# Graph attention and experts on one core: the query product of the second edge layer moves between a slot's two additions, and GpSimd gets 2 steps of 16

## What is computed

```python
Q = (enh @ Wq + bq).reshape(N, H, D); K = ...; V = ...      # H = 4 heads of D = 64
rel = rel_w[edge_relations]
mod_k = K[src] + 0.2 * rel[:, None, :]
scores = jnp.einsum('ehd,ehd->eh', Q[dst], mod_k) / D ** 0.5
seg_max = jax.ops.segment_max(scores, dst, num_segments=N)
ex = jnp.exp(scores - seg_max[dst])
denom = jax.ops.segment_sum(ex, dst, num_segments=N)
agg = jax.ops.segment_sum(ex / denom[dst] * V[src], dst, num_segments=N)
```

## Time and profile before

| what | value |
|---|---|
| median of 3 runs | 1919.19 us (1916.95 to 1919.61) |
| the profiled execution | 1912.22 us |
| its span, first to last instruction | 1910.5 us |
| busy over the span | DVE 1426.3 us (75%), PE 1321.5 (69%), POOL 1012.8 (53%), ACT 925.1 (48%) |
| second edge layer, first to last multiplication L1335 | 1003.2 to 1589.4 us |

### The profile page before, as it was taken

How to read it: one execution, slowest core, us unless ns; L and a number is a source line. 1 busy time by engine, 2 the same in 40 slices (tenths; PEclk the granted TensorE clock), 3 DMA queues, 4 the chain that set the end, 5 groups by cost and what they waited for, 6 DMA issues and landing times. The chain is left out here.

```text
span 1910.5 us, 29161 instructions
## 1 busy us (share of the span) xinstructions
PE 1321.5 (69%) x7038; PEld 919.6 (48%) x7038; DVE 1426.3 (75%) x3659; ACT 925.1 (48%) x3196; POOL 1012.8 (53%) x1082
## 2 busy tenths in 40 slices
PE   5436655665665569998867778777878778563286
PEld 4324433443443457776544555555555554452164
DVE  5458888888988953436868899999999997776043
ACT  2444556555555343322440677777777773231033
POOL 2377777777776000000517777777777775101555
PEclk9767887787777759999986899999999999775599
DMA  5766767667666119000358888888888884325564
GB/s 121 202 175 203 207 200 215 206 207 217 210 208 186 56 30 356 3 1 6 138 199 260 268 265 251 265 261 265 269 261 269 263 266 139 110 69 109 187 192 137
DMA packets 174910, 356.04 MB, mean 186 GB/s; under 512 B 29303, under 2 KB 70825, under 8 KB 174621
## 3 DMA queue, kind: packets, MB, share of 16 engines
q0 software_dynamic: 58192, 175.85, 30.6%
q1 hardware_dynamic: 116558, 178.33, 29.8%
HBM read 268.46 MB, written 89.75 MB: 187 GB/s over the span
## 5 line engine op out<-in xcount | busy, mean ns | idle before, releaser
L796 POOL DMA_INDIRECT e_rows<-h_rows,src_col x416 | 412.9, 993 | 127.0 <-issue 123.6
L1282 POOL DMA_INDIRECT e_rows<-kv_rows,src_col x320 | 306.5, 958 | 99.9 <-issue 66.8
L1042 PE MATMUL e_sum<-e_rows,e_of_dst 128*128 128x264 f32 x832 | 291.1, 489 | 98.3 <-DVE e_rows L887 81.8
L1501 ACT ACTIVATE e_rows<-e_rows 128x64 f32<-128x64 f32 x1152 | 281.4, 335 | 0.3
L1564 PE MATMUL e_query<-q,e_to_dst 128*128 x1248 | 203.5, 294 | 78.3 <-DVE e_rows L1335 58.1
L1042 PEld LDWEIGHTS e_sum<-e_rows,e_of_dst 128*128 128x128 f32 x832 | 172.5, 235 | 141.5 <-DVE e_rows L887 88.9
L1604 PE MATMUL e_sum<-e_rows,e_of_dst 128*128 128x260 f32 x640 | 185.2, 412 | 1.8 <-POOL e_rows L1212 1.2
L1564 PEld LDWEIGHTS e_query<-q,e_to_dst 128*128 128x128 bf16 x1248 | 120.3, 100 | 134.0 <-issue 94.8
L969 ACT ACTIVATE e_rows<-e_rows 128x32 f32<-128x32 f32 x832 | 181.0, 305 | 0.1
L1423 DVE TENSOR_TENSOR acc<-acc,e_sum 128x260 f32 x346 | 145.4, 420 | 41.5 <-DVE acc L1423 20.4
L1282 POOL DMA_INDIRECT x<-kv_rows,src_col x96 | 91.5, 953 | 72.9 <-POOLq L2087 38.5
(11 more groups left out here) (415 smaller groups left out, 2676.0 us busy)
## 6 DMA issues: line engine op xcount, KB each, us to landing
step_of<-e_of_dst SPq DMA_DIRECT2D x104, 256.0 KB, 2.3
e_of_dst<-step_of SPq DMA_DIRECT2D x104, 256.0 KB, 3.7
sorted_rows<-zeros SPq DMA_DIRECT2D x1, 14560.0 KB
rows<-sorted_rows SPq DMA_DIRECT2D x56, 260.0 KB, 2.9
e_rel<-step_rel SPq DMA_DIRECT2D x26, 512.0 KB, 4.3
step_to<-e_to_dst SPq DMA_DIRECT2D x26, 512.0 KB, 5.9
e_to_dst<-step_to SPq DMA_DIRECT2D x52, 256.0 KB, 4.4
e_rows<-h_rows,src_col POOLq DMA_INDIRECT x416, 3.3
```

The source lines that it names most:

```text
L796: pool.indirect_dma_start(out=g[t // BATCH % R][:, t % BATCH, :], out_offset=None, in_=k.h_rows[:, :], in_offset=bass.IndirectOffsetOnAxis ...
L1042: pe.matmul(psm[t % NB], of_dst[q][:, s % GROUP, :], g[m % R][:, s, :], start=True, stop=True).then_inc(summed, 1)
L1282: pool.indirect_dma_start(out=rows_at(t, 1)[:, 0, :], out_offset=None, in_=k.kv_rows[:, :], in_offset=bass.IndirectOffsetOnAxis(ap=k.src_c ...
L1501: ins = act.activation(x, x, ACT.Copy, scale=row[:, plo + h:plo + h + 1])
```

## The change

Two things change in the DVE, ACT and POOL programs of the second edge layer; no operation of the computation is added or taken away.

1. `score_multiply(m + 1, q)` is written after `add(first, w)` and the piece of the maxima that follows it, and before `add(first + 1, w)`. It was written before both additions, the window load and the rescaling.
2. `by_pool` holds the steps 5 and 13 of each 16, where it held 3, 7 and 13. POOL adds 47 steps in place of 70, DVE 369 in place of 346. All of POOL's steps are second steps of a slot, before and after.

```diff
-    by_pool = [t for t in range(TAIL) if t % BATCH in (3, 7, 13)]
+    by_pool = [t for t in range(TAIL) if t % BATCH in (5, 13)]
...
                 if q % 8 == 5 and ahead < CHUNKS:
                     masks(ahead)
-                if more:
-                    score_multiply(m + 1, q)
                 if first >= 0 and first % 8 == 0:
                     w = load_windows(first, 8)
                 if q == 2 and m:
...
                 if first == m * LONG and m:
                     v.wait_ge(k.dve_steps, c.count)
                     rescale(m, w[0])
                 add(first, w)
                 if q == 2 and m:
                     fall_of_maximum(m, made)
                 elif q == 3:
                     made = maxima(made)
+                if more:
+                    score_multiply(m + 1, q)
                 add(first + 1, w)
```

## The result

| | before | after |
|---|---|---|
| median of 5 runs | 1919.61 us (1916.95 to 1924.81) | 1934.59 us (1933.98 to 1942.55) |
| span of the profiled execution | 1910.5 us | 1932.7 us |
| ratio after to before | | 1.0085, 95% interval 1.0064 to 1.0106 |

What follows compares the result with a forecast made beforehand. DVE paced the steady part; after the change a 2.79 us cycle through PE would. Eleven lots at +1.8 us (19), first lot +0.8, clock +1: +21 on 1912.2, 1933; median 7 above, 1940 us, range 1926 to 1960.

Steps and rivals of the forecast that it cites:

- The cycle is multiplication, query products, sum, addition, multiplication: Plain slots after the change: DVE and PE wait on each other in this order, 2.45 + 0.34 = 2.79 us each.
- the chain: From DVE's multiplication through PE's query products and first sum to the earliest first addition: 2.45 us, hidden before the change.
- The split pair: Two-addition slots on DVE: multiplication between the dependent additions, 2.48 us of own work in place of 2.78.
- DVE paces it: Steady part of the kernel before: DVE, busy 429.1 of 457.9 us (94%), was claimed to set the pace.
- The sum for a lot: One lot of 32 steps (16 slots), its three stretches added: +0.8 - 0.5 + 1.5 = +1.8 us.
- Slots 1 to 4: Stretch of a lot: additions moved, waits gone, 0.5 us newly exposed; 13.72 to 13.2 us, -0.5.
- slots 5 and 6: Stretch of a lot with corrected sum and rescaling: 5.33 to 6.8 us, +1.5.
- rescaling near its upper bound: Slot 6: rescaling put 1.1 us behind the reduction for two register set-ups; slot 3.6 us, bounds 3.2 and 3.8.
- the allowance for the half-rate clock: Some 27 us of the stretch ran at 1.2 GHz, where the cycle is 3.6 us: 1 us added.
- waits for sums: DVE's first additions in plain slots wait for PE: 0.3 to 0.65 us some 150 times, 60 to 75 us in all.
- The additions given back: The 23 additions moved from POOL to DVE cost nothing extra, lying where DVE would wait longer without them.
- rival c: PE, waiting more, gets the half clock more often; a quarter of 186 slots adds 37 us: 1977 us, chance 0.09.

Runs made afterwards that it cites:

- pool_only: Kernel before, its DVE order kept, with POOL adding steps 5 and 13 of 16 in place of 3, 7 and 13: 1922.14 us, ratio 1.0007.
- order_only: Changed kernel with POOL's steps 3, 7 and 13 of 16 as before, so only the multiplication's place differs from before: 1933.86 us, ratio 1.0075.

## Why the prediction came out right, step by step

**The mechanism.** "The cycle is multiplication, query products, sum, addition, multiplication", put at 2.79 us in every plain slot, is what the timeline shows: 2.78, with and without a POOL step, and 2.79 as the mean of the 100 plain slots of ten lots. The 2.45 from multiplication to addition are 2.44. The run with the sum ahead of the query products takes the chain away and turns the loss into a gain; the longer and the shorter chain move the slot by what arrives at the addition, as far as DVE's own 2.46; and both edits of PE's program that were made on the kernel before, where the chain hides, change it by 0.2% at most.

**Own work.** The split pair saves what the rows said, 0.3 us in a slot with two additions, once the chain is out of the way: such a slot takes 2.45 us, against 2.76 before. The Trainium skill (VectorE: DVE Perf Modes, The DRAIN you can't avoid) says that a semaphore costs nothing on top of the pipeline's emptying. These rows disagree: the 0.3 us is the price of an addition that waits for the one directly ahead of it. "DVE paces it" was too simple. `pool_only` gave DVE 23 additions more in the old order and cost nothing that can be told, so its waits for POOL's additions and for gathers were part of the pace.

**The sum for a lot.** Predicted +1.8 us, measured 47.56 - 46.13 = +1.43, as means of ten lots. The prediction read one lot of the kernel before. Its whole, 46.13 us, happens to be the mean, but its parts are not:

| slots | predicted: before, after | mean of ten lots: before, after |
|---|---|---|
| 7 to 15 and 0 | 27.08, 27.9 | 26.96, 27.90 |
| 1 to 4 | 13.72, 13.2 | 13.54, 13.38 |
| 5 and 6 | 5.33, 6.8 | 5.63, 6.28 |

The plain slots were met. Slots 1 to 4 were put 0.2 us too low, slots 5 and 6 0.5 us too high, and there a term was mis-sized. I put rescaling near its upper bound, 1.1 us behind the reduction, because it needs two register set-ups. It came 0.60 behind:

```profile
1249.89 0.68 DVE L1341 TENSOR_REDUCE e_scores<-e_rows 128x8 f32<-128x512 f32 x1
1250.49 0.15 DVE L1411 SCALAR_TENSOR_TENSOR acc<-e_fac,acc 128x4 f32 x1
1250.56 0.41 DVE L1412 SCALAR_TENSOR_TENSOR acc<-e_fac,acc 128x256 f32 x1
1251.01 0.42 DVE L1423 TENSOR_TENSOR acc<-acc,e_sum 128x260 f32 x1
```

Nothing is idle ahead of it: the trace has both set-ups at 1250.0 and 1250.1, while the reduction ran. The kernel before already said as much in a row that stands between those of the earlier trace rows:

```profile
1243.80 0.68 DVE L1335 TENSOR_TENSOR e_rows<-e_rows,e_query 128x512 f32<-128x512 f32 x1
```

There the rescaling, at 1244.40, starts 0.60 after this multiplication, which is the bare price of a pass. From rescaling to addition it is now 0.52 us in place of 0.69. So slot 6 took 3.0 us, under even the lower bound of 3.2. Slot 5, with its wait of 0.45 for the corrected sum, took 3.2.

Over the layer the sum was +21 us and the stage gave +15.8. Of the 5 us, 4 lie in the whole lots (15.3 measured, 19.3 put), 1 in the allowance for the half-rate clock and the rest in the first lots. The measured median is 5.4 us under the 1940 for the same reason. The whole lots would be further off if slots 1 to 4 had not been put too low: those two errors offset each other in part, which is luck.

**Waits.** I expected 60 to 75 us of waits for sums in some 150 places. Up to the last multiplication the profile lists 41.7 us in 132, of which 34.7 in 113 in the ten lots. I had counted from start to start, and the list counts idle time only, some 0.08 us less each time; that is a little over half of the difference to the 60, and the fewer places are most of the rest. PE's waits for the multiplication are each about as long as predicted (median 0.61 us before, 0.59 after), but there are more of them: 96.1 us in 147 of the 160 slots of ten lots, against 63.1 us in 94. The prediction's "PE waits in nearly every slot today" was an over-reading; it waited in three of five.

**The additions given back** cost nothing, as predicted: `order_only` and the changed kernel agree. What I did not see is that they would have cost nothing in the old order either, since what DVE waited for POOL and gathers took about as much. The half-rate clock (rival c) does not explain the loss: the steady part was granted 0.99 of full, before 0.97. Lots with the full clock throughout took 45.74 us before (5 of them) and 47.18 after (6), +1.44, the same as over all ten.

## What to carry to other kernels

Before moving an instruction ahead of or behind a waiting one on an in-order engine, follow the semaphore that it raises: here the multiplication frees a bank, the bank's next user stands in PE's queue ahead of the sum, and the moved instruction now waits for that sum. Add up such a ring from the trace and compare it with the slot; whether a ring hides behind an engine that is 94% busy turns here on a few tenths of a microsecond. And when a reordering loses to a ring, look at the other engine's order as well: here the same change with one line moved on PE is 1.3% faster than the kernel before. It needs both of its parts: the same line moved on the kernel before gives nothing, and with POOL's old share the gain is 0.2%. The old DVE order with two POOL steps and the line moved was not run.

## What was not expected of the hardware

- Three more query products on PE, with the same operands as the three before them, lengthened the way from the first product to the sum by 0.23 us (0.80 to 1.03), where I had put 0.41 from six products in 0.82. The addition that waits for the sum started 0.16 us later.
- The same three products on the kernel before made it no slower but 0.2% faster, with TensorE's clock granted at full in the ten lots in place of 0.97.
- DVE's queue ran its register set-ups ahead while a pass was under way: two of them (1250.0 and 1250.1) and a load of window numbers (1249.1, 0.60 us long) were hidden under other work in slot 6.
- An engine's help can cost more than it saves while no engine is full: with three steps of 16 POOL was 77% busy, and ten lots lasted 11 us longer than with two steps, where it was 76% busy.
